# The router of each batch moved into the attention of the next batch, and the first experts' combine rows loaded batch by batch

## The chip, the cores and the metric

One core of one Trainium2 chip runs the program. The metric is device time in microseconds (us) of one execution. TensorE (PE) multiplies, VectorE (DVE), ScalarE (ACT) and GpSimd (POOL) work elementwise, and SyncE (SP) issues all DMAs here. Each engine takes its instructions in the order of its own list; between engines semaphores order the work.

## What is computed

The input is x with 4 batches of 512 tokens and 128 features. Per batch, a conditioning vector gives shift, scale and gate (mod). The block is an attention with 16 heads of 64 and a relative position bias, then a mixture of 160 experts (inner size 64, the best 8 per token) with one shared expert:

```python
h = _layernorm(x) * (1 + ca) + sa
x = x + ga * attention(h)              # softmax(q k^T / 8 + bias[rel]) v, then o_w
h = _layernorm(x) * (1 + cb) + sb
probs = sigmoid(h @ router_w.T + expert_bias)
top_w, top_idx = top_k(probs, 8)
top_w = top_w / (sum(top_w) + 1e-09) * 2.5
combine[token, top_idx] = top_w        # 160 columns per token
h1 = silu(h @ w_gate[e].T)             # every expert, every token
routed = sum over e of (h1 * combine[:, e]) @ w_down[e].T
shared = silu(h @ w_gate_shared.T) @ w_down_shared.T
x = x + gb * (routed + shared)
```

## The kernel before

**Attention.** Batches go one after another, and in a batch the 16 heads go in 8 pairs. The function `pair(b, n)` exists once per engine; n counts pairs from 2 to 9 in a loop over batches, so that pairs 8 and 9 of batch b are pairs 0 and 1 of batch b+1. A pair has 8 units: 2 heads times 4 tiles of 128 queries. For a unit TensorE computes the scores (L409, L411), VectorE adds the bias and takes the row maximum (`add_bias`, L975), ScalarE takes the exponential (L706), VectorE inverts the sums (L992), GpSimd normalises (L858), TensorE transposes (L420) and ScalarE or VectorE copies the transposed tile to `PT` (L204; units 0, 2, 4, 6 ScalarE, the odd ones VectorE). `attend` (L433) multiplies with the values, `copy_o` (L998) evacuates, `project_out` (L446) applies the output weights. `project_qk(b, n + 2)` (L383) at the end of pair n and `project_v` (L394) in its middle fill PSUM banks 0 and 1 (`BANK_PROJ`); `qk_high` (ScalarE, L702) and `qk_low` (VectorE, L958) split the queries and keys into a high and a low part, and six DMAs on SP spread them for the scores. Banks 2 and 3 hold scores, 4 and 5 transposed tiles, 6 the attention output, 7 the projected output.

The order of every engine in a pair is written by hand. For TensorE it is: scores 0 and 1; attend (key blocks 2 and 3 of pair n-2); transposes 4 and 5 of pair n-1; scores 2 and 3; values; output projection; transposes 6 and 7; scores 4 and 5; attend (blocks 0 and 1 of pair n-1); transposes 0 and 1; scores 6 and 7; queries and keys of pair n+2; transposes 2 and 3. At pair 2 of a batch VectorE also adds the attention output of the batch before to x (L1018) and takes the statistics of its layer norm (L1010).

**Router.** After the attention of all four batches, the whole router runs for all tokens: moments and 1/deviation (L1092, L676, L891), norm (L895), transposes (L530), shift and scale on ScalarE (L775), logits (L538, L540), sigmoid (L781), transposes back (L553, L554), `keep_top` on VectorE (L1107 to L1127: the 8 largest, their sum, the other probabilities set to zero), scaling (L798, L1137), transposes of the combine weights (L569, L571), copies (L804, L805) and a store to `comb_rows` in memory (L323). The shared expert (L591, L809, L603) starts the accumulation in PSUM banks 0 to 3.

**Experts.** Two experts form one pair of 128 inner rows, so there are 80 pairs, and each is done for two halves of 1024 tokens: 160 steps. A step is a gate product (6 matmuls of 128x512 in two PSUM banks, three passes of high and low parts), SiLU on ScalarE (L830), the multiplication by the combine rows on VectorE (L1163), a split in high (ScalarE, L822) and low (VectorE, L1150), and a down product (6 matmuls) that TensorE runs three steps later (`LAG`). All 12 matmuls have the line L620. Four expert pairs form a round; weights and combine rows are in rings of four. The rows of an expert pair are read from `comb_rows` by two DMAs of 512 KB, each broadcast over 64 partitions (L313).

**Names in the lists of instructions.** `qk_low` is the semaphore of L958, `v_copied` that of the copied values, `copied_by_dve` and `copied_by_act` those of L204, `pv_done` that of attend, `biased` that of L975.

## Time and profile before

| | us |
|---|---|
| median of 3 runs | 1000.38 (1000.25 to 1002.1) |
| the profiled execution | 999.45 |
| its span, first to last instruction | 997.2 |
| TensorE busy | 946.7 (95%) |
| VectorE busy | 767.4 (77%) |
| ScalarE busy | 678.3 (68%) |
| GpSimd busy | 398.2 (40%) |

Attention takes the span up to 500.1 us, the router and shared expert the stretch up to 542 us, and the experts the rest. Share of busy time is an average over stages: GpSimd works only in attention. In a timeline row, the first number is the start in us from the span's start, the second the busy time in us, then engine, line, operation, output<-input, shape and count; the bracket at the end is the idle time of the engine just before and what ended it. TensorE matmuls overlap in such rows, so the time that a group costs is read from start to start.

### The profile page before, as it was taken

Reading aid. Unit: us, or ns where it says so; the run is one execution under the profiler, and the core shown is the slowest. Engines: PE = TensorE matmul, PEld = TensorE weight load, DVE = VectorE, ACT = ScalarE, POOL = GpSimd, SP = SyncE. Lnnn points to the kernel's source line nnn. Section 1 sums busy time; section 2 is a strip of 40 time slices with the busy share of each in tenths; the row PEclk is TensorE's granted clock in tenths of the full one; section 3 lists DMA queues with packets and bytes.
Section 4 is the critical chain, followed back from the end, with each engine's and each line's share of the span. In section 5 each row is a group of like instructions: output and inputs, shape, how many; then the busy total and the mean of one; then the engine's idle time right before and its main releaser. Section 6 shows DMA issues by size and latency. Waiting matters only on the chain.

```text
span 997.2 us, 15699 instructions
## 1 busy us (share of the span) xinstructions
PE 946.7 (95%) x4592; PEld 685.8 (69%) x4592; DVE 767.4 (77%) x1452; ACT 678.3 (68%) x1168; POOL 398.2 (40%) x260
## 2 busy tenths in 40 slices
PE   4889999999999999999979699999999999999997
PEld 2546666666666666666524578888888888888886
DVE  5757667766676666767546689999999999999997
ACT  4656666666666666666536577777777777777775
POOL 0668888888888888888800000000000000000000
PEclk9999999999999999999979899999999999999999
DMA  7985445445553564355002999999999999999991
GB/s 210 274 224 125 97 118 127 117 95 128 128 120 81 117 149 110 82 128 127 22 0 75 213 218 221 220 220 223 222 221 225 221 222 223 222 222 222 222 208 43
DMA packets 71105, 160.57 MB, mean 161 GB/s; under 512 B 10272, under 2 KB 36192, under 8 KB 60944
## 3 DMA queue, kind: packets, MB, share of 16 engines
q1 hardware_dynamic: 71056, 159.97, 71.2%
q8 instruction: 24, 0.39, 0.2%
q14 instruction: 25, 0.20, 0.1%
HBM read 105.60 MB, written 2.42 MB: 108 GB/s over the span
## 4 chain that ended last, share of the span: by engine, by line
PE 84%; DMA 5%; DVE 4%; ACT 2%; POOL 2%; SPq 1%; issue 1%; POOLq 0%; ACTq 0%; DVEq 0%
PE ps L620 40%; PE ps L433 11%; PE ps L420 10%; PE ps L409 5%; PE ps L411 5%; PE ps L383 4%; PE ps L446 2%; PE ps L394 2%; POOL prob L858 2%; DMA strips<-in_L_ffn_w_down 2%; DMA k_low<-qk 2%; DVE prob L975 1%; DMA strips<-comb_rows 1%; DMA comb_rows<-strips 1%; PE ps L538 1%
## 5 line engine op out<-in xcount | busy, mean ns | idle before, releaser
L858 POOL TENSOR_SCALAR prob<-prob,rinv 128x512 f32<-128x512 f32 x256 | 398.1, 1568 | 96.4 <-DVE rinv L992 94.3
L706 ACT ACTIVATE prob<-prob,nmax 128x512 f32<-128x512 f32 x256 | 182.9, 715 | 139.5 <-DVE nmax L975 139.5
L620 PE MATMUL ps<-hT,wT 128*128 128x512 f32 x960 | 243.9, 390 | 0.3 <-DVE wT L1144 0.3
L1163 DVE TENSOR_TENSOR PT<-v_sb,strips 128x1024 f32<-128x1024 f32 x160 | 195.9, 1224 | 43.1 <-ACT v_sb L830 29.3
L830 ACT ACTIVATE v_sb<-ps 128x1024 f32<-128x1024 f32 x160 | 164.4, 1028 | 65.2 <-PE ps L620 65.1
L620 PE MATMUL ps<-stack,wT 128*128 128x512 f32 x640 | 198.4, 392 | 9.5 <-DVE wT L1150 9.5
L620 PEld LDWEIGHTS ps<-hT,wT 128*128 128x128 f32 x960 | 180.5, 188 | 38.9 <-ACT strips L805 1.1
L1150 DVE TENSOR_TENSOR wT<-PT,stack 128x1024 fp32r<-128x1024 f32 x160 | 195.0, 1219 | 0.0
L204 DVE COPY PT<-ps 128x512 f32<-128x512 f32 x128 | 88.5, 691 | 137.9 <-PE ps L420 135.2
L822 ACT CAST stack<-PT 128x1024 fp32r<-128x1024 f32 x160 | 166.6, 1041 | 9.5 <-DVE PT L1163 9.5
L420 PEld LDWEIGHTS ps<-ident,prob 128*128 128x128 f32 x1024 | 114.4, 140 | 75.9 <-POOL prob L858 50.9
L975 DVE CUSTOM_DVE_ANT_0 prob<-ps,strips 128x512 f32<-128x512 f32 x256 | 164.5, 680 | 2.7 <-PE ps L411 2.1
L620 PEld LDWEIGHTS ps<-stack,wT 128*128 128x128 f32 x640 | 120.1, 189 | 36.7 <-DVE wT L1150 12.1
L420 PE MATMUL ps<-ident,prob 128*128 128x128 f32 x1024 | 137.2, 276 | 2.8 <-ACT PT L204 1.6
L433 PE MATMUL ps<-PT,v_sb 128*64 128x512 f32 x512 | 124.4, 607 | 4.3 <-ACT PT L204 3.4
L409 PE MATMUL ps<-stack 128*128 128x512 f32 x256 | 112.7, 440 | 6.0 <-DMA k_low<-qk 5.8
L620 PE MATMUL ps<-wT 128*128 128x512 f32 x320 | 98.9, 391 | 0.0
L204 ACT COPY PT<-ps 128x512 f32<-128x512 f32 x128 | 74.0, 578 | 19.1 <-PE ps L420 19.0
L433 PEld LDWEIGHTS ps<-PT,v_sb 128*64 128x64 f32 x512 | 31.5, 137 | 64.7 <-issue 49.7
L620 PEld LDWEIGHTS ps<-wT 128*128 128x128 f32 x320 | 60.3, 189 | 12.6
L409 PEld LDWEIGHTS ps<-stack 128*128 128x128 f32 x256 | 48.8, 191 | 13.0 <-issue 4.0
L817 ACT CAST wT<-strips 128x256 fp32r<-128x256 f32 x80 | 32.3, 405 | 34.1 <-DMA strips<-in_L_ffn_w_down 33.9
(105 smaller groups left out, 742.8 us busy)
## 6 DMA issues: line engine op xcount, KB each, us to landing
strips<-comb_rows SPq DMA_DIRECT2D x158, 512.0 KB, 12.3
stack<-qk SPq DMA_DIRECT2D x128, 256.0 KB, 3.9
k_low<-qk SPq DMA_DIRECT2D x64, 128.0 KB, 3.9
hT<-qk SPq DMA_DIRECT2D x64, 128.0 KB, 3.8
strips<-bias_rows SPq DMA_DIRECT2D x3, 1792.0 KB, 14.7
strips<-in_L_ffn_w_gate SPq DMA_DIRECT2D x80, 64.0 KB, 10.4
strips<-in_L_ffn_w_down SPq DMA_DIRECT2D x80, 64.0 KB, 12.3
strips<-bias_rows SPq DMA_DIRECT2D x2, 896.0 KB, 5.3
```

What stands on the lines that cost most here:

```text
L204: return copy(dst[:, :, qt * P:(qt + 1) * P], ps[:, BANK_T + u % 2, :].rearrange("p (k s) -> p k s", s=P))
L409: nc.tensor.matmul(ps[:, BANK_S + g % 2, :], stack[:, par, head, 0, qt * P:(qt + 1) * P], stack[:, par, head, 1, :], start=True, stop=False)
L420: last = nc.tensor.transpose(ps[:, BANK_T + u % 2, kb * P:(kb + 1) * P], prob[:, u, kb * P:(kb + 1) * P], ident[:, :])
L433: last = nc.tensor.matmul(ps[head * HD:(head + 1) * HD, BANK_O, :], v_sb[:, (n // 2) % 2, kb, (n % 2) * P + head * HD:(n % 2) * P + (head ...
L620: last = nc.tensor.matmul(ps[:, bank + c, :], weights(a), rows(m, c), start=start and k == 0, stop=stop and k == 2, skip_group_check=True)
L706: nc.scalar.activation(prob[:, u, :], prob[:, u, :], ACT.Exp, bias=nmax[:, u:u + 1], scale=-1.0, accum_out=rsum[:, u:u + 1]).then_inc(s_ex ...
L822: nc.scalar.copy(h_high[:, k % 4, :], weighted[:, k % 4, :]).then_inc(s_hh, 1)
L830: nc.scalar.activation(silu[:, k % 2, :], ps[:, BANK_G + 2 * half:BANK_G + 2 * half + 2, :].rearrange("p c s -> p (c s)"), ACT.Silu).then_ ...
L858: nc.gpsimd.tensor_scalar(prob[:, u, :], prob[:, u, :], rinv[:, u:u + 1], None, ALU.mult).then_inc(s_prob, 1)
L975: nc.vector.tensor_tensor_reduce(out=prob[:, u, :], in0=ps[:, BANK_S + u % 2, :], in1=backwards, scale=-1.0, scalar=3.0e38, op0=ALU.add, o ...
L1150: nc.vector.tensor_tensor(h_low[:, k % 4, :], weighted[:, k % 4, :], h_high[:, k % 4, :].bitcast(F32), ALU.subtract).then_inc(s_hl, 1)
L1163: nc.vector.tensor_tensor(weighted[:, k % 4, :], silu[:, k % 2, :], cb[:, r, half * HALF:(half + 1) * HALF], ALU.mult).then_inc(s_mul, 1)
```

## The change

The router of batch b-1 runs inside the attention of batch b (`route = b - 1`), in pairs 2 to 7, in PSUM bank 0 or 1 by the pair's number (`router_bank`). Only that of the last batch runs after attention, and there it is written between the first expert products. The first eight steps are reordered: first the token half 0 of four expert pairs, then half 1 (`step_of_first`). The combine rows of these four are loaded in three parts: half 0, then batch 2, then batch 3. The deviation is inverted on GpSimd by a power of -0.5. Shift and scale go to VectorE. The shared expert's gate product uses split operands, 3 matmuls instead of one at full precision. `kLow` gets a buffer of its own for both parities.

```diff
@@ sync
+                    if n == HPAIRS + 1 and b >= 1:
+                        store_comb(b - 1)
                     stack_pair(b, n + 2)
...
-            sp.wait_ge(s_ttr, B * G)
+            sp.wait_ge(s_ttr, (B - 1) * G + UNITS * 6)
             for r in range(DEPTH):
                 load_weights(0, r)
...
+            sp.wait_ge(s_cst, 64)
+            for r in range(DEPTH):
+                load_rows(0, r, slice(0, HALF), s_first_rows)
+            store_comb(B - 2)
+            sp.wait_ge(s_cst, 32 * (B - 1))
+            for r in range(DEPTH):
+                load_rows(0, r, slice(HALF, HALF + S), s_first_rows)
+            store_comb(B - 1)
             sp.wait_ge(s_cst, 32 * B)
-            load_rows(0, 0, slice(HALF, T))
-            for r in range(1, DEPTH):
-                load_rows(0, r)
+            for r in range(DEPTH):
+                load_rows(0, r, slice(HALF + S, T))
@@ tensor
+            def bank_free(b, n):
+                last = b == B - 1
+                pe.wait_ge(s_qkl, b * HPAIRS + (min(n + 2, HPAIRS) if last else n + 2))
+                pe.wait_ge(s_vc, b * HPAIRS + (min(n + 1, HPAIRS) if last else n + 1))
...
             def pair(b, n, final=False):
+                route = b - 1 if b >= 1 else None
                 scores(b, n, 0)
                 scores(b, n, 1)
+                if route is not None and n == 4:
+                    bank_free(b, n)
+                    logits(route, router_bank(n), 0)
+                    logits(route, router_bank(n + 1), 1)
+                if route is not None and n == 5:
+                    bank_free(b, n)
+                    transpose_sigmoids(route, router_bank(n), 0)
+                if route is not None and n == 6:
+                    bank_free(b, n)
+                    transpose_sigmoids(route, router_bank(n), 1)
+                if route is not None and n == 7:
+                    bank_free(b, n)
+                    transpose_comb(route, router_bank(n), 0)
                 if n >= 2:
                     attend(b, n - 2, 2)
                     attend(b, n - 2, 3)
...
+                if route is not None and n == 3:
+                    bank_free(b, n)
+                    transpose_normed(route, router_bank(n))
...
             pe.wait_ge(w_split, 6)
             pe.wait_ge(ld["ow"], 16)
+            pe.wait_ge(ld["small"], 80)
             for b in range(B - 1):
                 for n in range(2, HPAIRS + 2):
                     pair(b, n)
@@ scalar, pair
                 exponential(b, n, 0)
                 exponential(b, n, 1)
+                if route is not None and n == 4:
+                    sigmoids(route, (router_bank(n), router_bank(n + 1)))
...
                 exponential(b, n, 6)
                 exponential(b, n, 7)
+                if route is not None and n == 3:
+                    h2_high(route)
                 if not (final and n >= HPAIRS - 2):
                     qk_high(b, n + 2)
@@ vector, pair
                 add_bias(b, n, 0)
                 add_bias(b, n, 1)
+                if route is not None and n == 3:
+                    norm2(route)
+                if route is not None and n == 4:
+                    h2_low(route)
...
                 add_bias(b, n, 2)
                 add_bias(b, n, 3)
+                if route is not None and n == 2:
+                    moments(route)
+                if route is not None and n in (5, 6):
+                    keep_top(route, router_bank(n), n - 5)
                 if n >= 1:
                     copy_probs(b, n - 1, 7)
@@ vector, after attention
+            first_weigh(0)
+            modulate2(late, ROUTER_A)
+            first_weigh(1)
+            product_low(0, 0)
+            h2_low(late)
+            first_weigh(2)
+            product_low(0, 1)
+            first_weigh(3)
+            product_low(0, 2)
+            keep_top(late, ROUTER_A, 0)
+            keep_top(late, ROUTER_B, 1)
+            product_low(0, 3)
+            first_weigh(4)
+            first_weigh(5)
```

TensorE at the start of pair 5 of batch 1, before. The first four rows are the scores of units 0 and 1, L433 is attend, L420 a transposed unit of the pair before:

```order
L409 MATMUL ps<-stack 128x512 [waits biased,stack_odd]
L411 MATMUL ps<-hT,stack 128x512
L409 MATMUL ps<-stack 128x512 [waits biased]
L411 MATMUL ps<-hT,stack 128x512
L433 MATMUL ps<-PT,v_sb 64x512 x4
L420 MATMUL ps<-ident,prob 128x128 [waits copied_by_act,normalised]
```

The same place in the changed kernel, where L501 and L502 transpose sigmoids:

```order
L432 MATMUL ps<-stack 128x512 [waits biased,stack_odd]
L434 MATMUL ps<-kLow,stack 128x512
L432 MATMUL ps<-stack 128x512 [waits biased]
L434 MATMUL ps<-kLow,stack 128x512
L501 MATMUL ps<-ident,router_rows 128x128 [waits sigmoid,v_copied,qk_low]
L502 MATMUL ps<-ident,router_rows 128x32
L501 MATMUL ps<-ident,router_rows 128x128
L502 MATMUL ps<-ident,router_rows 128x32
L456 MATMUL ps<-PT,v_sb 64x512 x4
```

Four transposes stand ahead of attend, and the first of them waits for `qk_low`. In pairs 4 and 7 the logits and the combine transposes stand at this place behind the same wait.

VectorE in the same pair, from the bias of unit 2 to the copy of transposed unit 7, before:

```order
L975 ISA prob,nmax<-ps,strips 128x512 [waits scores,transposed]
L975 ISA nmax 128x1
L975 ISA prob,nmax<-ps,strips 128x512 [waits scores,transposed]
L975 ISA nmax 128x1
L204 COPY PT<-ps 128x4x128 [waits transposed]
L992 RECIPROCAL rinv<-rsum 128x2 [waits normalised,exped]
```

And in the changed kernel, from behind the bias of unit 3:

```order
L1147 MAX top8<-ps 128x8 [waits h2_low,logits,probs_transposed]
L1147 MAX top8<-ps 128x8
L1153 TENSOR_REDUCE tsum<-top8 128x2 [waits dve_step]
L1151 MATCH_REPLACE router_first<-top8,ps 128x160
L1156 TENSOR_SCALAR tsum<-tsum 128x2 [waits dve_step]
L1151 MATCH_REPLACE router_first<-top8,ps 128x160
L1159 RECIPROCAL tsum<-tsum 128x2 [waits dve_step]
L1162 TENSOR_SCALAR tsum<-tsum 128x2 [waits dve_step]
L1164 TENSOR_TENSOR router_first<-ps,router_first 128x320 [waits dve_step]
L1168 TENSOR_SCALAR router_first<-router_first,tsum 128x160 [waits top_kept]
L1168 TENSOR_SCALAR router_first<-router_first,tsum 128x160
L208 COPY PT<-ps 128x4x128 [waits transposed]
```

Eleven instructions of half a `keep_top` now stand ahead of the copy (L208, L204 before); pair 6 has the other half.

TensorE behind the last attend of the last batch, before, where L446 is the output projection, L453 the transposed attention output and L530 the transposed norm:

```order
L446 MATMUL ps<-oT,woT 128x512 [waits o_copied]
L453 MATMUL ps<-ident,yT 128x128 [waits y_gated]
L453 MATMUL ps<-ident,yT 128x128 x3
L530 MATMUL ps<-ident,PT 128x128 [waits xn_done,ld_small,biased]
L530 MATMUL ps<-ident,PT 128x128 x3
```

In the changed kernel, from behind the transposed attention output (L617 shared down product, L632 gate product, L488 transposed norm, L494 logits):

```order
L617 MATMUL ps<-prob,wdsT 128x512 [waits shared_silu] x2
L632 MATMUL ps<-hT,wT 128x512 [waits weights_split]
L632 MATMUL ps<-hT,wT 128x512 x5
L488 MATMUL ps<-ident,PT 128x128 [waits normed2]
L488 MATMUL ps<-ident,PT 128x128 x3
L632 MATMUL ps<-hT,wT 128x512 [waits weights_split]
L632 MATMUL ps<-hT,wT 128x512 x5
L494 MATMUL ps<-PT,routerT 128x512 [waits modulated2]
L494 MATMUL ps<-PT,routerT 32x512 [waits modulated2]
```

The expert products now start ahead of and between the router steps of the last batch.

## Rows read from the trace of the kernel before

**Rows 1.** Busy time by stretch; columns are length, engines, TensorE's granted clock, DMA share, GB/s.
```profile
200.00:300.00 100.00, 99.88 (x551) 65.85 (x550) 69.60 (x190) 65.65 (x153) 86.16 (x56) 1.00 0.50 118
...
500.10:542.00 41.90, 33.03 (x118) 14.79 (x118) 27.18 (x123) 22.73 (x42) 0.00 (x0) 0.88 0.05 16
...
555.60:560.00 4.40, 4.39 (x12) 3.43 (x12) 2.11 (x3) 1.39 (x2) 0.00 (x0) 0.58 1.00 216
```

**Rows 2.** Timeline at the start of pair 2 of batch 0, and one DMA issue.
```profile
61.01 0.76 PE L409 MATMUL ps<-stack 128*128 128x512 f32 x1 [3.74 <-DMA k_low<-qk]
...
69.98 0.43 SPq L291 DMA_DIRECT2D ebias<-in_L_ffn_expert_bias  x1
```

**Rows 3.** DMA issues by tensor: count, KB each, median us from issue to landing.
```profile
ebias<-in_L_ffn_expert_bias SPq DMA_DIRECT2D x1, 0.1 KB, 3.2
```

**Rows 4.** Timeline at the start of a pair in steady attention.
```profile
349.05 0.99 ACT L702 CAST qk<-ps 128x1024 fp32r<-128x1024 f32 x1
349.13 0.48 PE L409 MATMUL ps<-stack 128*128 128x512 f32 x1
...
350.09 1.20 DVE L958 TENSOR_TENSOR qk<-ps,qk 128x1024 fp32r<-128x1024 f32 x1
...
350.22 1.94 PE L433 MATMUL ps<-PT,v_sb 128*64 128x512 f32 x8
```

**Rows 5.** Timeline of TensorE in the router, before.
```profile
519.72 1.13 PE L538 MATMUL ps<-PT,routerT 128*128 128x512 f32 x2
...
521.75 0.33 PE L553 MATMUL ps<-ident,strips 128*128 128x128 f32 x1
...
523.49 1.13 PE L538 MATMUL ps<-PT,routerT 128*128 128x512 f32 x2
...
537.97 0.60 PE L569 MATMUL ps<-ident,strips 128*128 128x128 f32 x4
...
538.84 0.60 PE L569 MATMUL ps<-ident,strips 128*128 128x128 f32 x4
```

**Rows 6.** Timeline of steady attention at the copy of transposed unit 7.
```profile
342.41 0.69 DVE L204 COPY PT<-ps 128x512 f32<-128x512 f32 x1 [1.39 <-PE ps L420]
...
343.23 1.94 PE L433 MATMUL ps<-PT,v_sb 128*64 128x512 f32 x8
```

**Rows 7.** Timeline of VectorE in the router: the best eight of batch 0, the scaling of two batches.
```profile
517.80 1.03 DVE L1107 MAX8 PT<-ps 128x8 f32<-128x160 f32 x4 [6.49 <-PE ps L554]
...
520.48 0.82 DVE L1127 TENSOR_TENSOR strips<-ps,strips 128x640 f32<-128x640 f32 x1
...
534.38 1.78 DVE L1137 TENSOR_SCALAR strips<-strips,tsum 128x160 f32<-128x160 f32 x8
```

**Rows 8.** Timeline of ScalarE at the change of its function table, with the copy ahead.
```profile
526.72 0.61 ACT L792 CAST hT<-PT 128x512 fp32r<-128x512 f32 x1
...
527.35 1.28 ACT L809 ACT_TABLE_LOAD   x1
...
528.65 1.17 ACT L809 ACTIVATE prob<-ps 64x512 f32<-64x512 f32 x2
```

**Rows 9.** Timeline from the last attend to the end of the last product.
```profile
500.14 0.69 DVE L998 COPY oT<-ps 128x512 f32<-128x512 f32 x1 [3.79 <-PE ps L433]
...
508.38 2.05 PE L530 MATMUL ps<-ident,PT 128*128 128x128 f32 x8 [4.87 <-DVE PT L895]
...
539.25 0.34 SPq L323 DMA_DIRECT2D comb_rows<-strips  x1
...
546.73 1.23 DVE L1163 TENSOR_TENSOR PT<-v_sb,strips 128x1024 f32<-128x1024 f32 x1 [4.50 <-DMA strips<-comb_rows]
...
555.61 1.22 PE L620 MATMUL ps<-stack,wT 128*128 128x512 f32 x2 [7.74 <-DVE wT L1150]
...
990.34 1.03 PE L664 MATMUL ps<-ident,prob 128*128 128x128 f32 x8
```

**Rows 10.** The page's groups, experts: busy us, mean ns of one, idle before.
```profile
L830 ACT ACTIVATE v_sb<-ps 128x1024 f32<-128x1024 f32 x160 | 164.4, 1028 | 65.2 <-PE ps L620 65.1
```

More of the change, by code:

```diff
@@ new lines, in logits, with transpose_sigmoids @@
+            def logits(b, bank, part):
+                pe.wait_ge(s_h2, b + 1)
+                rows, weights = ((slice(0, P), routerT[:, 0:P]), (slice(0, E - P), routerT[:, P:E]))[part]
+                nc.tensor.matmul(ps[rows, bank, :], weights, h2[b], start=True, stop=True).then_inc(s_lg, 1)
+            def transpose_sigmoids(b, bank, part):
+                pe.wait_ge(s_sig, 2 * (b + 1))
+                for t in range(2):
+                    at = ps[:, bank, t * E:(t + 1) * E]
+                    n = (2 * part + t) * P
+                    nc.tensor.transpose(at[:, 0:P], probsT[:, n:n + P], ident[:, :])
+                    last = nc.tensor.transpose(at[:, P:E], probsT2[:, n:n + P], ident[0:E - P, 0:E - P])
+                last.then_inc(s_back, 1)
@@ L456, in pair, with transpose_comb @@
+            def transpose_comb(b, bank, part):
+                pe.wait_ge(s_comb, b + 1)
+                rows, cols = ((slice(0, P), slice(0, P)), (slice(0, E - P), slice(P, E)))[part]
+                for t in range(QT):
+                    last = nc.tensor.transpose(ps[rows, bank, t * P:(t + 1) * P], comb[b][:, t, cols], ident[:, :])
+                last.then_inc(s_ctr, 1)
             def pair(b, n, final=False):
+                route = b - 1 if b >= 1 else None
                 scores(b, n, 0)
@@ new lines, in round_of @@
+                    product_high(i, k - 1)
+                    if weights is not None:
+                        if k == 0:
+                            act.wait_ge(s_d, ROUND - 2)
+                        if k in weights:
+                            weights_high(*weights[k])
+                    elif half == 1 and not (final and r >= DEPTH - 2):
+                        weights_high(i + (r + 2) // DEPTH, (r + 2) % DEPTH)
+            late = B - 1
+            shared_silu(0)
+            shared_silu(1)
@@ new lines, in _ @@
+            gate_silu(0, 0)
+            gate_silu(0, 1)
+            product_high(0, 0)
+            h2_high(late)
+            sigmoids(late, (ROUTER_B, ROUTER_A))
+            gate_silu(0, 2)
+            product_high(0, 1)
+            gate_silu(0, 3)
+            product_high(0, 2)
+            gate_silu(0, 4)
+            product_high(0, 3)
+            gate_silu(0, 5)
+            copy_comb(late, ROUTER_A, 0)
+            copy_comb(late, ROUTER_B, 1)
+            shared_silu(2)
+            shared_silu(3)
@@ L1147, in product_low @@
+            moments(late)
+            variance_eps(late)
+            norm2(late)
             def product_low(i, k):
@@ L1172, in _ @@
[L1172 to L1177 removed]
+                    weigh(i, k, r, half)
+                    product_low(i, k - 1)
+                    if weights is not None:
+                        if k in weights:
+                            weights_low(*weights[k])
+                    elif half == 1 and not (final and r >= DEPTH - 2):
+                        weights_low(i + (r + 2) // DEPTH, (r + 2) % DEPTH)
```

530 lines of the change are left out of this document (284 added, 246 removed).

## Prediction

> **What bounds the kernel now.** I read the busy time by stretch first, then the timeline of one attention pair, then the passage from attention to the experts. In steady attention TensorE is busy 99.88 of 100 us, GpSimd 86, VectorE 70, ScalarE 66 [rows 1]. That TensorE is full is seen in the starts, not in the busy share: the scores of two units start at 349.13 and attend at 350.22, so four matmuls of 512 columns take 1.09 us and nothing lies between them and the next group [rows 4]. The other engines wait for it once or twice per pair, VectorE for example 1.39 us ahead of the copy of unit 7 [rows 6]. So anything put on TensorE in attention costs its full length, and so does any wait in TensorE's list. Between 500.1 and 542 TensorE is busy 33 of 41.9 us, with dependent steps, at a mean clock of 0.88 of full [rows 1]; after two gate steps and a third it stands still 7.74 us for the first combine rows and runs its first 4.4 us behind that at 0.58 [rows 1, 9]. From 555.61 it is full to 990.34, which is 317 products (2 for each of 160 steps, less the 3 gates already done), 1.371 us each [rows 9]. This passage is what the change is after.
>
> **Part 1, the wait for the small tensors.** `ld["small"]` counts the router's and shared expert's weights and the bias. Before, TensorE asked for them after attention. Now it asks ahead of pair 2 of batch 0. That pair starts at 61.01, after a wait for keys [rows 2]. The last of the five loads is issued at 69.98 and its tensor takes 3.2 us to land, hence 73.2 [rows 2, 3]. These loads stand on SP behind the spreading of pair 3's queries and keys, which doesn't depend on pair 2, so they come no earlier or later than now. Everything behind the wait is attention itself: no engine has scores to work on. Cost 73.2 - 61.0 = **12.2 us**. Bounds: 9.0 if it landed at once, 12.6 with the issue's own 0.43 on top.
>
> **Part 2, router products inside attention.** Per batch, start to start: four transposes of the norm 0.44 (half of the eight combine transposes, 0.87), logits 521.75 - 519.72 = 2.03, sixteen transposes of sigmoids 523.49 - 521.75 = 1.74, combine transposes 0.87 [rows 5]. Sum 5.1. Three batches 15.2; of the last the combine transposes fall in its pair 7, where GpSimd is behind and TensorE waits anyway, so **14.4 us**.
>
> **Part 3, the wait for `qk_low`.** In pairs 4 to 7 the router's step stands right behind scores 0 and 1 and waits until the bank is read out. The scores end 1.09 us into a pair; the split of queries and keys runs from 350.09 to 351.29, 2.16 us into it [rows 4]. So TensorE stands 1.07 us, with attend queued behind it. It can't be earlier: ScalarE's cast at 349.05 only starts when the last exponential of the pair is through [rows 4]. In pair 3 `h2_high` (a cast of 128x512, 0.61 [rows 8]) is put ahead of that cast, so pair 4 waits 1.7. Batches 1 and 2: 4 x 1.07 + 0.6 = 4.9 each. Batch 3: pair 7 has no new queries and keys, 3.8. Sum **13.6 us**.
>
> **Part 4, `keep_top` ahead of a copy.** In pairs 5 and 6 VectorE does half of it behind the bias of unit 3. For four tiles the chain ran from 517.80 to 521.30, 3.5 us, and scaling a tile takes 1.78 / 8 = 0.22 [rows 7]. Half of the tiles can't take less than half, 1.75 + 0.44 = 2.2, nor more than 3.5 + 0.44 = 3.9. I take 2.7, since the maxima and the last subtraction halve and the small dependent steps stay. VectorE has 1.39 us idle there [rows 6], and 0.2 more because attend came later. The copy of unit 7 ends 343.10 and attend starts 343.23 [rows 6]: no slack. So TensorE waits 1.1 each, six times: **6.7 us** (3.5 to 13).
>
> **Part 5, small things in attention.** Norm on VectorE in pair 3 (four tiles), the low part of h2, shift and scale and moments fall in VectorE's idle times of 1.39 us and longer; without these gaps they would cost 2.3 us per batch (four tiles at 0.22, two passes of 0.69 [rows 6, 7]). The power on GpSimd is not in the trace; it lies between nothing and a normalise step, and GpSimd has 14% free, so 0. On ScalarE two table loads per batch of 1.28 us each: a copy ends 527.33, the load starts 527.35 and the next function at 528.65, one load costs 1.30 with nothing around it [rows 8]. They stand in pair 4, which TensorE has already stretched by 3.7 us, and eat that. The four weight splits in pair 7 of batch 3 sit between exponentials on which a GpSimd without slack waits. For all this 1.0 us (0 to 4).
>
> The Trainium skill, in "ScalarE: Activation LUTs", section "What ACT_TABLE_LOAD costs", gives 1.283 us for the load and 1.380 us more for a drain. The load agrees with row 527.35, the drain isn't in rows 8. By the page pair 4 would be late by 2 x 1.38 = 2.8 us in each of three batches, and the sum 8 us higher; see the second rival.
>
> **Part 6, the passage.** Take T as the end of the last attend, 500.1. Before, norm transposes started at T+8.3 [rows 9]; the shared gates now ahead of the projection cost 0.6, moments of one batch instead of four save as much, so T+8. Then `first_weigh(0)` (1.23 [rows 9]) stands ahead of `modulate2` on VectorE: logits T+10.6 to 12.6. ScalarE comes with SiLU 1, a cast and `h2_high` (1.03, 1.03, 0.6 [rows 8, 10]), loads the sigmoid table, does two activations of 0.7 (the cast of that size took 0.61 [rows 8]), loads the SiLU table, and SiLU 2 is done at T+17.9. VectorE then needs two multiplications and two low parts, 4 x 1.23, to T+22.8, two halves of `keep_top` to T+28.3 and `product_low(3)` to T+29.5. TensorE has run out of work at T+24.5 and waits for that: 5 us. Down 3, combine transposes and two copies end T+32.8. From the issue of a store to the multiplication by loaded rows it took 546.73 - 539.25 = 7.5 us [rows 9]; now with smaller loads I take 7.0: T+39.8. Two multiplications, then low part 4, T+43.5: TensorE, with all eight gates done, waits 4 us. The next weights are split behind four more VectorE steps and 0.4: T+48.8, another wait of 4 us. From there TensorE is full, with 8 gates and 5 downs done, so 307 products x 1.371 = 420.9 follow. That ends at T+469.7. Before: 990.34 - 500.1 = T+490.2. Gain **20.5 us**. Bounds: if all three waits vanished 33; if each grew by half and the clock fell once more as at 555.6 (4.4 us at 0.58), 12.
>
> **Sum.** 12.2 + 14.4 + 13.6 + 6.7 + 1.0 = 47.9 in attention, minus 20.5, is +27.4. Span 997.2 + 27.4 = 1024.6; the profiled execution took 2.25 more than its span, 1026.9, and the median of the runs lies 0.93 above the profiled one: **1027.8 us**, which I round to 1028.
>
> **Rivals.**
> 1. *TensorE has room in attention* (faster). If its matmuls are pipelined and the 99.9% is only how they look, the products of part 2 and the waits of parts 3 and 4 are swallowed. LDWEIGHTS is busy 65.85 of 100 us there [rows 1]. Then 12.2 + 1 - 20.5 = -7.3, 993 us. The change is faster from the point where less than 7.3 of the 34.7 us of parts 2 to 4 shows. Against it: start-to-start times of 0.27 us per matmul and no idle time between groups [rows 4]. The Trainium skill names this trap ("Perfetto Trace Analysis", section "Identifying the Most-Contended Engine": judge TensorE by weight-load busy share, not by matmul busy share), and by it attention would have a third of TensorE free. Chance 0.07.
> 2. *ScalarE breaks pair 4.* If the stretch of pair 4 doesn't cover the two table loads, the exponentials of units 2 and 3 come late by 2 x 1.28 = 2.6 us, then the copies and attend: 7.7 more over three batches, 1036. For it: ScalarE waits for the logits in the same place. Against it: the 3.7 us by which TensorE is late there. Chance 0.12.
> 3. *The waits of parts 3 and 4 are made up.* TensorE gives its followers time at the start of a pair, and if something else than TensorE were late in a pair, that time would come back. -20, 1008. VectorE and ScalarE do wait for TensorE in each pair, so I don't believe it. Chance 0.12.
> 4. *The small loads land in time* (the wait isn't what it says): 1016. Chance 0.06.
> 5. *The passage goes better or worse than walked*, -13 to +9 as bounded: 1015 to 1036, with the forecast's sign; chance of being off by over 8 us 0.13.
>
> **How the numbers follow.** Forecast 0.50, rivals as given. Range: from rival 3 and the best passage to rival 2 with a little more, 1012 to 1039, leaves out rival 1 and most of rival 3. A measurement of this kernel can tell about 0.2% from no change. Faster 0.07, same 0.03 (parts 2 to 4 shrunk to a fifth), slower 0.90.
>
> **What would show it.** A TensorE idle time of about 16 us in the first 75 us of the span, where 3.7 stands now. In pairs 4 to 7 of batches 1 to 3 an idle TensorE of 1.1 us ahead of router steps, ended by the split of queries and keys; in pairs 5 and 6 another of about 1 us ahead of attend, ended by VectorE's copy. The last attend at about 500 + 47 = 547 instead of 500. Experts full from about 596. I am wrong if pairs with router steps grow by no more than their products, or if the last attend ends before 530.

## The result, and the profile after

The change makes the kernel slower: 1034.67 us is the median of four runs (1034.07 to 1044.02), 1001.24 us that of four runs of the kernel before. The ratio is 1.035, with a 95% interval of 1.029 to 1.042. The forecast was 1028 us, slower, with a range up to 1039. The profiled execution of after took 1034.07 us, its span 1031.3, where before it had 999.45 and 997.2. So 34.1 us of span are to be explained, and the walk of the prediction had 27.4.

The page of after, its first lines:

```profile
span 1031.3 us, 15705 instructions
## 1 busy us (share of the span) xinstructions
PE 949.7 (92%) x4596; PEld 689.1 (67%) x4596; DVE 781.3 (76%) x1487; ACT 688.3 (67%) x1161; POOL 402.4 (39%) x265
```

TensorE does 3.0 us more work than before (946.7), but its share falls from 95% to 92%: what was added is mostly standing still. Busy time by stretch, with the columns of [rows 1] (length, PE, PEld, DVE, ACT, POOL, granted clock, DMA share, GB/s), for 60 to 75 us, two stretches of attention and the passage:

```profile
60.00:75.00 15.00, 0.16 (x1) 0.19 (x2) 2.46 (x9) 1.50 (x2) 2.32 (x2) 0.56 0.84 226
200.00:300.00 100.00, 91.99 (x498) 59.41 (x500) 66.98 (x192) 63.01 (x141) 76.58 (x51) 1.00 0.43 101
400.00:500.00 100.00, 95.23 (x520) 62.26 (x520) 68.18 (x186) 66.34 (x147) 81.40 (x54) 1.00 0.44 101
555.00:596.00 41.00, 32.79 (x121) 20.09 (x119) 21.15 (x53) 17.54 (x21) 1.04 (x1) 0.96 0.07 23
```

Where [rows 1] had 99.88 us of matmuls in 200 to 300, there are now 91.99. And from 60 to 75 us TensorE does next to nothing. The start of pair 2 of batch 0, against [rows 2] (the bracket is the idle time of the engine ahead of the row and what ended it):

```profile
62.42 1.01 ACT L751 CAST qk<-ps 128x1024 fp32r<-128x1024 f32 x1 [4.33 <-DMA kLow<-qk]
...
71.88 0.43 SPq L302 DMA_DIRECT2D ebias<-in_L_ffn_expert_bias  x1
74.84 0.77 PE L432 MATMUL ps<-stack 128*128 128x512 f32 x1 [16.51 <-DMA ebias<-in_L_ffn_expert_bias]
```

The keys of the pair have landed by 62.4, since ScalarE goes on there, and TensorE starts only at 74.84, when the small bias vector lands.

Two heads of router pairs in steady attention, and attend in the middle of the second (pairs 5 and 6 of batch 1); L501 and L502 are the transposes of sigmoids, L456 is attend, L417 the value projection:

```profile
240.99 0.33 PE L501 MATMUL ps<-ident,router_rows 128*128 128x128 f32 x1 [1.05 <-DVE qk L1045]
...
245.59 0.87 PE L417 MATMUL ps<-wT,hcur 128*128 128x256 f32 x6
...
258.75 0.33 PE L501 MATMUL ps<-ident,router_rows 128*128 128x128 f32 x1 [1.06 <-DVE qk L1045]
...
259.62 1.94 PE L456 MATMUL ps<-PT,v_sb 128*64 128x512 f32 x8
...
263.34 0.87 PE L417 MATMUL ps<-wT,hcur 128*128 128x256 f32 x6
...
268.38 1.94 PE L456 MATMUL ps<-PT,v_sb 128*64 128x512 f32 x8 [1.50 <-issue]
```

The value projection runs once per pair, so the distance between two of its starts (245.59 and 263.34: 17.75 us) is the length of a pair. Tables below use this interval. Before, it was 14.17 us in these pairs. The same stretch on VectorE and GpSimd, with half of `keep_top`:

```profile
263.48 3.11 POOL L934 TENSOR_SCALAR prob<-prob,rinv 128x512 f32<-128x512 f32 x2 [2.71 <-DVE rinv L1079]
...
264.50 0.56 DVE L1147 MAX8 top<-ps 128x8 f32<-128x160 f32 x2
...
266.12 0.48 DVE L1162 TENSOR_SCALAR tsum<-tsum 128x2 f32<-128x2 f32 x1
...
267.16 0.52 DVE L1168 TENSOR_SCALAR router_first<-router_first,tsum 128x160 f32<-128x160 f32 x2
267.60 0.69 DVE L208 COPY PT<-ps 128x512 f32<-128x512 f32 x1
```

The chain runs from 264.50 to the start of the copy at 267.60, 3.10 us. TensorE's waits in attention, grouped by line (180 to 555 us; busy, mean ns, then idle time ahead with what ended it):

```profile
L456 PE MATMUL ps<-PT,v_sb 128*64 128x512 f32 x384 | 92.8, 604 | 13.0 <-issue 9.8 <-ACT PT L208 3.1
...
L494 PE MATMUL ps<-router_first,routerT 128*128 128x512 f32 (+1 forms) x12 | 6.3, 625 | 4.7 <-DVE qk L1045 4.7
L501 PE MATMUL ps<-ident,router_rows 128*128 128x128 f32 x12 | 3.9, 328 | 6.7 <-DVE qk L1045 6.7
L509 PE MATMUL ps<-ident,router_first 128*128 128x128 f32 (+1 forms) x24 | 3.7, 278 | 2.1 <-DVE qk L1045 2.1
```

Three groups wait for `qk_low` (L1045), 13.5 us together. Of the 9.8 us called "issue" ahead of attend, 0.8 belong to the end of attention, where before has them too, and 9.0 are six waits of 1.50, in pairs 5 and 6 of three batches. The row at 268.38 shows what they are: the copy of unit 7 at 267.60 ends at 268.29, and attend starts behind it.

The passage, against [rows 9]:

```profile
554.57 0.69 DVE L1085 COPY oT<-ps 128x512 f32<-128x512 f32 x1 [3.79 <-PE ps L456]
...
560.76 1.04 POOL L943 TENSOR_TENSOR rstd<-mv,minus_half 128x4 f32<-128x4 f32 x1 [11.43 <-DVE mv L1116]
...
577.04 0.55 DVE L1147 MAX8 top<-ps 128x8 f32<-128x160 f32 x2
...
583.71 0.91 PE L632 MATMUL ps<-stack,wT 128*128 128x512 f32 x2 [4.42 <-DVE wT L1276]
...
588.48 0.34 SPq L305 DMA_DIRECT2D comb_rows<-router_rows  x1
...
594.88 1.23 DVE L1283 TENSOR_TENSOR PT<-v_sb,strips 128x1024 f32<-128x1024 f32 x1 [11.23 <-issue]
...
598.72 1.22 PE L632 MATMUL ps<-stack,wT 128*128 128x512 f32 x2 [3.67 <-DVE wT L1276]
...
603.59 1.65 PE L632 MATMUL ps<-hT,wT 128*128 128x512 f32 x3 [1.95 <-DVE wT L1175]
...
1024.49 1.03 PE L713 MATMUL ps<-ident,prob 128*128 128x128 f32 x8
```

The last attend ends at 554.5 (before: 500.1) and the last expert product at 1024.65, where the row at 1024.49 begins the final transposes (before: 990.5). So the two halves of the change can be read apart: attention 54.4 us longer, the passage with the experts 470.1 us for 490.4, 20.3 us shorter.

### The profile page after: what moved, and what is told of

It is laid out like the page before. It is cut to its first block and busy times, and to the rows that moved or that the text cites. A ratio compares the mean times of both kernels' runs of the same rounds, so it can differ in the third digit from the quotient of the medians.

```text
span 1031.3 us, 15705 instructions
## 1 busy us (share of the span) xinstructions
PE 949.7 (92%) x4596; PEld 689.1 (67%) x4596; DVE 781.3 (76%) x1487; ACT 688.3 (67%) x1161; POOL 402.4 (39%) x265
## 5 line engine op out<-in xcount | busy, mean ns | idle before, releaser
L632 PE MATMUL ps<-hT,wT 128*128 128x512 f32 x960 | 245.4, 392 | 1.9 <-DVE wT L1175 1.9
L632 PEld LDWEIGHTS ps<-hT,wT 128*128 128x128 f32 x960 | 180.4, 189 | 42.6 <-DVE wT L1175 2.9
L632 PE MATMUL ps<-stack,wT 128*128 128x512 f32 x640 | 199.2, 393 | 9.1 <-DVE wT L1276 9.1
L208 DVE COPY PT<-ps 128x512 f32<-128x512 f32 x128 | 88.3, 690 | 127.1 <-PE ps L443 126.0
L632 PEld LDWEIGHTS ps<-stack,wT 128*128 128x128 f32 x640 | 121.0, 190 | 35.9 <-DVE wT L1276 10.8
L456 PE MATMUL ps<-PT,v_sb 128*64 128x512 f32 x512 | 124.8, 609 | 13.8 <-issue 9.8
L432 PE MATMUL ps<-stack 128*128 128x512 f32 x256 | 113.2, 442 | 18.6 <-DMA ebias<-in_L_ffn_expert_bias 16.5
L434 PE MATMUL ps<-kLow,stack 128*128 128x512 f32 x256 | 101.8, 398 | 0.0
L632 PE MATMUL ps<-wT 128*128 128x512 f32 x320 | 99.8, 393 | 0.0
L208 ACT COPY PT<-ps 128x512 f32<-128x512 f32 x128 | 74.2, 580 | 32.3 <-PE ps L443 32.3
L456 PEld LDWEIGHTS ps<-PT,v_sb 128*64 128x64 f32 x512 | 32.2, 137 | 73.1 <-issue 59.9
L632 PEld LDWEIGHTS ps<-wT 128*128 128x128 f32 x320 | 60.9, 190 | 12.8
L432 PEld LDWEIGHTS ps<-stack 128*128 128x128 f32 x256 | 49.1, 192 | 25.7 <-issue 16.7
```

The costliest lines, as they stand in the source:

```text
L208: return copy(dst[:, :, qt * P:(qt + 1) * P], ps[:, BANK_T + u % 2, :].rearrange("p (k s) -> p k s", s=P))
L432: nc.tensor.matmul(ps[:, BANK_S + g % 2, :], stack[:, par, head, 0, qt * P:(qt + 1) * P], stack[:, par, head, 1, :], start=True, stop=False)
L456: last = nc.tensor.matmul(ps[head * HD:(head + 1) * HD, BANK_O, :], v_sb[:, (n // 2) % 2, kb, (n % 2) * P + head * HD:(n % 2) * P + (head ...
L632: last = nc.tensor.matmul(ps[:, bank + c, :], weights(a), rows(m, c), start=start and k == 0, stop=stop and k == 2, skip_group_check=True)
```

## Experiments

"Interval" is the distance of two value projections, "end of attention" that of the last attend. Times are medians; those of two or four runs scatter by 1% and more in some cases, so that the profile's intervals decide where a few microseconds matter. Each interval is read from one profiled execution of its run.

**The wait for the small tensors, alone.** Before, with the one wait added:

```diff
             pe.wait_ge(ld["ow"], 16)
+            pe.wait_ge(ld["small"], 80)
             for b in range(B - 1):
```

> The kernel before with one wait added: TensorE asks for the small tensors ahead of pair 2 of batch 0, nothing else is changed. Theory: 12.2 us more than before (73.2 less 61.0), about 1013. Rival (the loads land in time): no change, 1001.

Measured: 1015.85 us for 1001.22, ratio 1.014 (1.011 to 1.018), 14.6 us more for the 12.2 expected. The first interval is 33.86 us, for 20.08 in before and 33.21 in after; attention ends at 514.79, and what follows takes 490.9 us for 490.4. Of the 13.8 us by which the interval grew, 11.4 are the wait for the small tensors (pair 2 starts at 74.16, its keys had landed by 62.77), 1.1 are keys that landed later, and 1.3 lie behind the wait, where TensorE works at a granted clock of 0.50 from 74 to 80 us. This one line costs about as much as all the router's matmuls in attention (14.4).

**The small loads issued first.** After, with the five loads ahead of the first spreading of queries and keys:

```diff
+            sp.dma_start(routerT[:, :], router_t).then_inc(ld["small"], 16)
...
+            sp.dma_start(ebias[0:E - P, 1:2], expert_bias[P:E, :]).then_inc(ld["small"], 16)
             stack_pair(0, 0)
             load_strips(1)
```

> The changed kernel with one edit: the five small loads (router, shared expert, bias) are issued ahead of the first spreading of queries and keys instead of behind the fourth, so the wait ahead of pair 2 of batch 0 finds them landed. Theory (part 1 of the prediction): TensorE's idle time of 16.5 us there shrinks to the 4 us that the wait for keys takes anyway, and the time falls by 12.3 us, from 1034.7 to about 1022. Rival: the pair would have been late anyway by something behind the wait, or the earlier loads push other start-up DMAs back: fall of under 6 us.

Measured: 1023.53 us, first interval 21.81; 11.1 us less than after, for the 12 to 13 of a wait that is gone. The next run looks for the rest.

**The wait moved back instead.**

```diff
-            pe.wait_ge(ld["small"], 80)
             for b in range(B - 1):
                 for n in range(2, HPAIRS + 2):
+                    if b == 1 and n == 2:
+                        pe.wait_ge(ld["small"], 80)
```

> After with one line moved: TensorE waits for the five small loads ahead of pair 2 of batch 1, over 100 us later, not ahead of pair 2 of batch 0; the loads stay where they are. If the 13.1 us by which the interval between the first two value projections of the start grew (33.21 for 20.08) are the wait alone, the interval falls back to about 20.1 and the kernel to 1034.7 - 13.1 = 1021.6, some 2 us below the version that issued the loads earlier (interval 21.81, 1023.5). If the five loads hold up the start by filling the queue, whoever waits for them, it stays at 30 or more and the time within 3 us of 1034.

Measured: 1023.9 us, first interval 21.78, attention ends at 542.36 (12.2 earlier than in after). The interval is that of the version with early loads (21.81), so where the loads stand makes no difference once nothing waits for them, but it didn't go down to 20.08. Two rows at the start of pair 2 say why:

```profile
62.33 0.77 PE L432 MATMUL ps<-stack 128*128 128x512 f32 x1 [4.79 <-DMA kLow<-qk]
...
64.30 3.27 PE L456 MATMUL ps<-PT,v_sb 128*64 128x512 f32 x8
```

Before has this attend as follows:

```profile
62.98 2.61 PE L433 MATMUL ps<-PT,v_sb 128*64 128x512 f32 x8
```

TensorE waits 4.79 us for keys there, 3.74 in before [rows 2]. This isn't from the change: in before with the added wait ScalarE's cast behind the same keys starts at 62.60, after 4.96 us for 3.81 in before, and nothing ahead of it was edited. The keys' landing varies by more than a microsecond from one execution to another. The other 0.7 us is the slower attend: the granted clock is 0.50, the lower of TensorE's two levels (1.2 of 2.4 GHz), all the way from 62 to 66 us, where before is back at 0.90 from 64 to 66. In both it fell while TensorE stood waiting for the keys. The wait itself is worth 74.84 - 62.6 = 12.2 us in after, 62.6 being ScalarE's 62.42 and the 0.17 by which TensorE follows it in before.

**The router's products behind attend.**

```diff
-                if route is not None and n == 4:
-                    bank_free(b, n)
...
                 if n >= 2:
                     attend(b, n - 2, 2)
                     attend(b, n - 2, 3)
+                if route is not None and n == 4:
+                    bank_free(b, n)
```

> The changed kernel with one edit: in pairs 4 to 7 TensorE's router step with its wait for the bank stands behind attend (key blocks 2 and 3) instead of ahead of it. Theory (part 3): the bank is read out 2.2 us into a pair and attend ends at 2.96, so the wait is gone: 13.6 us less, about 1021; in pair 4 ScalarE's sigmoids come 1.9 us later and may give 0.5 us each back. Rival: the wait only moves to the next group (transposes 4 and 5, or values), fall of under 4 us.

Measured: 1025.48 us, attention ends at 544.14, 10.4 us earlier. The waits on L1045 are gone, but 3.1 of the 13.5 us came back, in pair 4. TensorE's groups, with the columns of before:

```profile
L456 PE MATMUL ps<-PT,v_sb 128*64 128x512 f32 x384 | 92.8, 604 | 14.9 <-issue 9.9 <-ACT PT L208 5.1
...
L417 PE MATMUL ps<-wT,hcur 128*128 128x256 f32 x132 | 19.4, 282 | 1.3 <-ACT router_rows L780 1.3
```

The value projection of pair 4 now waits 0.45 us for the second sigmoid, and attend 0.62 us for a ScalarE copy behind it, three times each. These are what the wait for `qk_low` had covered.

**Half of `keep_top` moved behind the bias of unit 5.**

```diff
-                if route is not None and n in (5, 6):
-                    keep_top(route, router_bank(n), n - 5)
                 if n >= 1:
                     copy_probs(b, n - 1, 7)
...
+                if route is not None and n in (5, 6):
+                    keep_top(route, router_bank(n), n - 5)
```

> The changed kernel with one edit: in pairs 5 and 6 VectorE does its half of the best-eight chain behind the bias of unit 5 instead of behind that of unit 3, so the copy of unit 7 no longer stands behind it. Theory (part 4): TensorE's wait ahead of attend, 1.5 us in each of six pairs, goes: 9 us less, about 1026. Rival: the wait moves to the transposes or scores that need the later copies, fall of under 3 us.

Measured: 1036.79 us. The expectation of 9 us less failed. The six waits of 1.50 ahead of attend are gone, as expected, and nothing was won: attention ends at 557.21, 2.7 us later than in after. TensorE's groups:

```profile
L456 PE MATMUL ps<-PT,v_sb 128*64 128x512 f32 x384 | 96.6, 626 | 4.1 <-ACT PT L208 3.2 <-issue 0.8
...
L501 PE MATMUL ps<-ident,router_rows 128*128 128x128 f32 x12 | 3.9, 328 | 9.7 <-DVE qk L1045 9.7
L509 PE MATMUL ps<-ident,router_first 128*128 128x128 f32 (+1 forms) x24 | 3.7, 278 | 4.1 <-DVE qk L1045 4.1
```

The waits for `qk_low` grew from 13.5 to 18.6 us with those of L494 (4.8). The chain now stands ahead of the biases of units 6 and 7, so the exponentials, the cast and `qk_low` come later, and the next pair's head waits for just these: 2.06 to 2.09 us for 1.06. So the intervals that hold half a `keep_top` shrink by only 0.43 us (17.33 for 17.76, 17.06 for 17.48), 2.6 in six, which is what the rival had said (under 3).

That nothing at all was left has a second cause. Attend's own busy time rose by 3.8 us, because TensorE's granted clock fell three times, once in each batch. The first time, with the columns of [rows 1] in the last row:

```profile
258.51 0.33 PE L501 MATMUL ps<-ident,router_rows 128*128 128x128 f32 x1 [2.09 <-DVE qk L1045]
...
259.38 3.24 PE L456 MATMUL ps<-PT,v_sb 128*64 128x512 f32 x8
...
260.00:262.00 2.00, 2.00 (x8) 0.33 (x4) 0.00 (x0) 0.61 (x2) 0.43 (x1) 0.50 1.02 249
```

The same attend took 1.94 us in after (at 259.62 there), where the granted clock is 1.00 from 180 us to the end of attention. From the start of attend to the next scores it is 4.36, 4.35 and 4.36 us in the three places for 2.71 or 2.72: 1.6 us each, 4.9 together. The falls come behind waits for `qk_low` of 2.09, 1.38 and 2.06 us, but a wait of 1.38 in after and three of 2.06 or 2.07 in this run had none behind them, so what brings them on is not shown. Less their 4.9 us, attention would have ended 2.2 us earlier than in after.

**All three edits together.** The two waits compete for the same time, so the third edit had to be seen with the second.

> The changed kernel with the three edits together: small loads early, router steps behind attend, best-eight chain behind the bias of unit 5. Theory: the three waits are independent, 12.3 + 13.6 + 9 = 35 us less, about 1000, that is level with the kernel before; what is left of attention's growth is the router's own products (14 us) against the 20 us won in the passage, so down to 995 if nothing else waits. Rival: they overlap, under 28 us less, over 1007.

Measured: 1005.52 us (ten runs; ratio to before 1.006, 1.002 to 1.009), attention ends at 527.68. That is 29.2 us less than after, for 35 if the three waits were independent and under 28 by the rival. With the router's products behind attend nothing waits for `qk_low` at the head of a pair, and now the move of `keep_top` pays: the intervals that hold it shrink from 16.63 and 16.20 us to 15.45 and 15.04, 1.2 each for 0.43 alone. The granted clock stays at 1.00 there too, from 180 us to the end of attention. So together it wins 7 of its 9 us.

**TensorE full or not.** The logits of each router computed twice.

```diff
+                    pe.wait_ge(s_h2, route + 1)
+                    nc.tensor.matmul(ps[:, router_bank(n), :], routerT[:, 0:P], h2[route], start=True, stop=True)
+                    nc.tensor.matmul(ps[0:E - P, router_bank(n + 1), :], routerT[:, P:E], h2[route], start=True,
+                                     stop=True)
                     logits(route, router_bank(n), 0)
```

> The changed kernel with the two logits products of pair 4 done twice (same operands, same banks; the first result is overwritten by the second, so the output is unchanged). Theory (part 2): TensorE is full in attention, each of three batches pays 2.03 us: 6.1 more, about 1041. Rival 1 (TensorE has room in attention and its busy time only looks full): no change, 1035.

Measured: the interval of this pair is 20.58, 20.59 and 20.60 us in the three batches, for 18.55 to 18.57 in after. That is +2.03 us each for products that take 2.03 us start to start [rows 5]. Attention ends at 560.32, 5.8 later. TensorE has no room at all in this place. The time, 1042.01 us (two runs, 1036.67 and 1047.35), isn't used: in the profiled execution the stage behind attention took 478.5 us for 470.1, though the code there is the same.

**ScalarE's table loads.** In attention the exponential in place of the sigmoid, which needs no other table; the router of batches 0 to 2 then computes another function.

```diff
-                                         ps[rows, banks[part], :], ACT.Sigmoid,
+                                         ps[rows, banks[part], :],
+                                         ACT.Sigmoid if b == B - 1 else ACT.Exp,
```

> The changed kernel with the router's sigmoid inside attention replaced by the exponential, which leaves out the two function-table loads per batch (the router of batches 0 to 2 then computes another function, so the expert weights of these differ; the work is the same). Theory (part 5): the loads lie beside TensorE's longer pair 4, so 0 to 1 us less, 1034 to 1035. Rival 2: exponentials of units 2 and 3 come late by 2.6 us and with them attend, 7.7 us less, 1027.

In after ScalarE's timeline has both loads around the sigmoids of batch 0:

```profile
225.75 1.28 ACT L780 ACT_TABLE_LOAD   x1
227.04 1.25 ACT L780 ACTIVATE router_rows<-ps,ebias 128x512 f32<-128x512 f32 x2
...
228.82 1.28 ACT L755 ACT_TABLE_LOAD   x1
```

Measured: the interval of pair 4 is 18.54 us (211.33 to 229.87) for 18.55 in after, with no table load in it; attention ends at 555.02 for 554.53. In after the loads cost nothing. (1042.83 us is the median of two runs, 1035.59 and 1050.07.)

**The passage.** With all three edits, the combine transposes ahead of the fourth down product:

```diff
-            first_down(3)
             pe.wait_ge(s_kept, 2 * B)
             transpose_comb(late, ROUTER_A, 0)
             transpose_comb(late, ROUTER_B, 1)
+            first_down(3)
```

> As the kernel with the three edits, and in the passage TensorE transposes the last batch's combine weights ahead of the fourth down product instead of behind it. The store of these weights waits on it and TensorE later waits for their rows. Theory: the fourth down product took 2.4 us at a lowered clock ahead of the transposes; the chain to the rows gets shorter by it, 1.5 to 3 us less than the kernel with three edits. Rival: rows come no earlier because loading sets the end: 0.

Measured: 1001.33 us (ten runs, before 1001.55; ratio 0.999, 0.996 to 1.002). From the last attend to the last product it takes 466.4 us for 470.4: 4.0 less, more than the 1.5 to 3 expected. The store of the combine weights is issued 29.9 us behind the last attend for 33.9: earlier by the down product and by VectorE's last low part, which isn't waited for any more and which the expectation had left out.

**The same with the late wait.**

> The late wait, the router's products behind the attend step, the best-eight chain behind the bias of unit 5, and the transposes of comb ahead of the fourth down product, all at once. Against the version at 1001.3 (interval 22.02 at the start, where the small loads were issued early) only the start differs: 22.02 - 20.08 = 1.9 us less, so about 999.4, a ratio to the kernel before of 0.998. It is level with before or up to 0.4% below it. If the theory of the start is wrong and the loads themselves cost the time, it is at 1009 or more.

Measured: 1000.3 us (twelve runs), ratio 0.998 (0.995 to 1.000); the first interval is 21.23. The expectation, 999.4, had taken the 20.08 of before for it.

**The tiny scaling.** In after, L1162 scales two sums per row by 2.5. It took 0.48 us in each of its six executions in attention, and 0.17 in the passage:

```profile
266.12 0.48 DVE L1162 TENSOR_SCALAR tsum<-tsum 128x2 f32<-128x2 f32 x1
...
578.58 0.17 DVE L1162 TENSOR_SCALAR tsum<-tsum 128x2 f32<-128x2 f32 x1
```

It ends at 266.60, and GpSimd's pair of normalise steps at 263.48 + 3.11 = 266.59; the other five show the same within 0.02 us (for example 248.84 and 248.82). So it stands until GpSimd is through. The Trainium skill says this in "SBUF — State Buffer", section "SBUF: two separate sides": VectorE and GpSimd share one pair of ports, whoever has it holds it for a whole instruction, and VectorE asks for it only in some forms of instruction. The trace agrees in that this instruction ends with GpSimd's; that it is the ports for which it waits, no run here shows. The edit folds it into the two that follow:

```diff
-                then(nc.vector.tensor_scalar(scales, scales, ROUTED, None, ALU.mult))
...
-                                                   tsum[:, 1, n:n + 1], None, ALU.mult)
+                                                   tsum[:, 1, n:n + 1], ROUTED, ALU.mult, ALU.mult)
```

> After with the instruction that scales two sums by 2.5 (L1162, 128x2) folded into the two that scale the kept probabilities. In the profile of after it took 0.48 us each of six times in attention and ended within 0.02 us of the end of GpSimd's normalise pair, and 0.17 us in the passage, where GpSimd does nothing. Half a keep_top then takes 3.1 - 0.5 = 2.6 us in attention. If this chain sets the wait ahead of attend in pairs 5 and 6, that wait falls from 1.5 to 1.0 us, six times: about 3.0 us less, 1034.7 - 3.0 - 0.4 in the passage = 1031.3. Rival: the next instruction that reads and writes SBUF alone (the scaling of 160 columns) takes over the wait for GpSimd or something else is late there: the wait stays at 1.5 and the time within 1 us of 1034.7.

Measured: 1033.48 us (four runs, 1027.62 to 1036.17, too wide for 3 us), but the trace is clear. VectorE's chain ahead of the copy, GpSimd, and attend in pair 6 of batch 1:

```profile
262.97 3.10 POOL L934 TENSOR_SCALAR prob<-prob,rinv 128x512 f32<-128x512 f32 x2 [2.71 <-DVE rinv L1079]
...
264.01 0.56 DVE L1147 MAX8 top<-ps 128x8 f32<-128x160 f32 x2
...
265.62 0.49 DVE L1163 TENSOR_TENSOR router_first<-ps,router_first 128x320 f32<-128x320 f32 x1
266.14 0.52 DVE L1167 TENSOR_SCALAR router_first<-router_first,tsum 128x160 f32<-128x160 f32 x2
266.57 0.68 DVE L208 COPY PT<-ps 128x512 f32<-128x512 f32 x1
...
267.36 1.51 PE L456 MATMUL ps<-PT,v_sb 128*64 128x512 f32 x6 [0.97 <-issue]
```

The chain takes 2.56 us for 3.10, TensorE waits 0.97 for 1.50, and attention ends 3.6 us earlier, at 550.96. The chain does set this wait, one to one.

**The best version with this fold.**

> The version at 1000.3 us (late wait, router behind attend, best-eight chain later, comb transposes ahead of the down product) with the same fold. There the chain no longer stands ahead of the copy of unit 7, and TensorE waits behind it only some 0.3 us ahead of the projection of queries and keys: at most 0.3 x 6 = 1.8 us in attention and 0.4 in the passage, so 998.5 to 1000. Ratio to the kernel before 0.996 to 0.998.

Measured: 997.99 us (twelve runs) for 1002.62, ratio 0.9946 (0.991 to 0.998). This one is faster than both kernels, if only by 0.5% of before. Its two stages: attention ends at 520.83, 20.7 us later than before, and the rest takes 466.1 us, 24.3 less. The intervals of one batch, in us; the column "work" is 14.17 and the added products by themselves, start to start [rows 5]:

| pair to pair | before | work | after | router behind attend | all three | best with fold |
|---|---|---|---|---|---|---|
| 3 to 4 | 14.17 | 16.64 | 18.55 | 17.52 | 17.52 | 17.50 |
| 4 to 5 | 14.17 | 15.04 | 16.20 | 15.85 | 15.85 | 15.85 |
| 5 to 6 | 14.16 | 15.04 | 17.75 | 16.63 | 15.45 | 15.07 |
| 6 to 7 | 14.17 | 14.61 | 17.48 | 16.20 | 15.04 | 14.64 |
| 7 to 8 | 14.17 | 14.61 | 14.69 | 14.67 | 14.66 | 14.69 |

In the last column three of five pairs grow by their products and at most 0.1 us more. What is left stands in pair 4, behind the sigmoids on ScalarE:

```profile
213.94 0.98 PE L417 MATMUL ps<-wT,hcur 128*128 128x256 f32 x6 [0.45 <-ACT router_rows L781]
...
218.19 1.94 PE L456 MATMUL ps<-PT,v_sb 128*64 128x512 f32 x8 [0.60 <-ACT PT L208]
```

## Why the prediction was right, and by how much it wasn't

The direction, the two halves and four of the six parts came out as walked; the total is 6.7 us short (34.1 for 27.4 of span), nearly all of it in attention (54.4 for 47.9).

**Part 1** (12.2): the wait measured 12.2. The start is longer by 2.0 us beyond it (the value projection of pair 2 is at 81.58 for 67.39): the value projection before it is at 48.37 for 47.31 already, the keys come another 0.5 later, and 0.4 is the first attend behind the wait at the lower clock. The edited before, with 0.6, 1.1 and 1.3 for these three, shows that the router isn't their cause. The prediction had no term for them, and a single profile can't show how much they vary. The upper bound of 12.6 was too tight for what two profiles show; that the wait costs its full length was right.

**Part 2** (14.4): right. The doubled logits cost 2.03 us per batch, the half of the sigmoid transposes takes 259.62 - 258.75 = 0.87. With it falls rival 1: weight loads are busy 59 to 66% of the time in attention, and still no matmul fits in. The Trainium skill's page "Perfetto Trace Analysis", section "Identifying the Most-Contended Engine", judges TensorE's headroom by the busy share of weight loads (and by the work done against the peak); by that share a third of attention would be free, as rival 1 had it. Here the start-to-start times decide.

**Part 3** (13.6): 13.5 measured, 1.05 or 1.06 us at a head as walked (once 1.38) and 1.57 in pair 4 for the 1.7 taken. Moving the products behind attend removed it, but only 10.4 us came off.

**Part 4** (6.7): the mechanism was right and the term mis-sized, 9.0 measured. (Its bounds of 2.2 and 3.9 us for the chain make 3.6 to 14, not the 3.5 to 13 written there.) The step that failed is "I take 2.7" for the chain. 2.70 us is what half a `keep_top` takes in the passage (from 577.04 to the next at 579.74). In attention it takes 3.10, mostly since L1162 stands behind GpSimd. The rows for this term were taken from the router, where GpSimd is idle, and used in a stage where it is busy 86% [rows 1]. 3.10 less 1.39 and 0.2 is 1.5, the measured wait.

**Part 5** (1.0): table loads nothing, as forecast, but for a reason that depends on part 3: as soon as the wait for `qk_low` is gone, pair 4 waits 0.45 and 0.6 us behind the sigmoids; the reason is argued from this and not shown for the loads themselves. Rival 2 is refuted for after. For the versions without that wait it is open: no run there leaves the loads out. The Trainium skill, in "ScalarE: Activation LUTs", section "What ACT_TABLE_LOAD costs", adds a drain of 1.38 us to each load. The trace doesn't show one here: the load at 225.75 takes 1.28 us and the sigmoid starts at 227.04, and the pair's interval is the same within 0.01 us without any load. The power on GpSimd, not in the trace before, takes 1.04 us for 128x4 (560.76). The other growth of the attention, 3.3 us between the first value projection of pair 2 and the last attend beyond parts 2 to 4 (40.2 less 14.4, 13.5 and 9.0), lies in tenths over 15 intervals; 0.6 of it are three waits of 0.2 for a ScalarE copy. The rest stays open. So the 6.5 us by which attention was missed are 2.3 from part 4, 2.0 from the start, and 2.3 from here.

**Part 6** (20.5): 20.3 measured. The three waits were put at 5, 4 and 4 us and are 4.42, 3.67 and 1.95; the norm came later than walked (its transposes at T+8.5 for T+8; the power on GpSimd takes 1.04 us of the chain to it), and TensorE is steady at T+49.1 for T+48.8. That the walk went well is partly that its errors cancelled.

**Rival 3**, that waits are made up in a pair, is refuted by the intervals, which grow by every wait. The move of `keep_top` alone shows time handed from one wait to another. Rival 4 is refuted by the row at 74.84.

What the prediction didn't see is how the parts depend on each other. It priced each wait as if removing it would give its time back; 13.5 gave 10.4, and 9.0 gave 2.6 in the intervals alone and about 7 together with the other edit. Nor did it have the granted clock in attention: three falls, 4.9 us, turned that gain of 2.6 into a loss of 2.7.

## What to carry to other kernels

A stage whose bottleneck engine is full has no room to hide work in: every product and every wait that was put there cost its full length here, and moving work into it pays only if the work is placed where all its waits are already over. After removing a wait, look for what it had covered before counting the gain, and try edits of waits on the same chain together. When an edit wins nothing, read the granted clock of the stretch before calling the idea wrong. Take the duration of an instruction from a stage in which its neighbours are as busy as in the stage it moves to.

## What the runs showed of the hardware

A TENSOR_SCALAR of 128x2 on VectorE, SBUF to SBUF, took 0.17 us with GpSimd idle and 0.48 us beside GpSimd's normalise steps, six times of six ending within 0.02 us of GpSimd's instruction. The other one of this size (L1156) took 0.24 for 0.16, RECIPROCAL and MATCH_REPLACE8 in the same chain the same in both places (0.15 and 0.31).

Eight attend matmuls of 128x512 took 1.94 us at a granted clock of 1.00 and 3.24 where it fell to 0.50 (run with `keep_top` moved alone, 259.38); each such fall in attention cost 1.6 us.

A power of 128x4 elements on GpSimd took 1.04 us, two thirds of a normalise step of 128x512 (1.56).

A table load on ScalarE took 1.28 us, and two of them per batch in a covered place cost nothing that shows (interval 18.54 without, 18.55 with them).
